# Attention queries from five products, the head sum from rounded parts, and steps of two units

## The chip, the cores and the metric

The kernel runs on one core of one Trainium2 chip. A core has five engines with a queue of instructions each, which they work off in order: TensorE (PE, matrix products), VectorE (DVE), ScalarE (ACT), GpSimd (POOL) and SyncE (SP, which here only issues DMAs). They wait for each other through semaphores. The measure is the device time of one execution in microseconds (us); lower is better.

## The reference, cut to what matters

Four layers follow each other: a state space layer (Mamba), a sparse feed forward layer, a latent attention layer, and a clustered dense layer. The change touches the attention layer. It has 4 sequences of 256 tokens, 32 heads, query latents of 192 and key/value latents of 64 numbers per token:

```
q_c = hidden_size @ Wq_c.T + bq_c
q = (q_c @ Wq_up.T + bq_up).reshape(b, s, NH, Q_HEAD).transpose(0, 2, 1, 3)
kv = hidden_size @ Wkv_c.T + bkv_c
kv_nope, kv_rope = (kv[..., :KV_LORA], kv[..., KV_LORA:])
kvu = (kv_nope @ Wkv_up.T + bkv_up).reshape(b, s, NH, QK_NOPE + V_HEAD).transpose(0, 2, 1, 3)
k_nope, v = (kvu[..., :QK_NOPE], kvu[..., QK_NOPE:])
```

Scores are softmaxed over the keys, the heads' outputs are summed over the heads, and Wo projects the sum.

## The kernel before, in words

Activations lie with features on partitions and the 1024 tokens along the free axis, in halves of 512 (h). Most products are split: an operand is kept as a rounded part (type fp32r, "high") and a rest ("low"), and three fast products, high with high, low with high, high with low, take the place of one plain f32 product. `split` writes such threes; its matmuls are L583, L584, L585.

The attention layer works on 16 pairs of heads (i). For a pair, `fold` (L884) multiplies the up projections of queries and keys (four products 128x64, L890), so that scores can be made against the key latents themselves; ACT copies the result into lAB (L1359), rounds it into lABh (L1362), and POOL makes lABl (L507). `query` (L894) makes, per head of the pair and half of the tokens (j = 0 to 3, four per pair, 64 in all), a 128x512 tile of queries from 192 latents and a row of ones that carries the bias: a three over 128 rows and a three over 65 rows, six products. ACT rounds it (L1367), DVE makes its low part (L1761). All but one of the queries use the PSUM bank A, so a query waits until the one before is evacuated.

A unit (w) is one head on one sequence; a pair has 8 units (v = w modulo 8), so there are 128 units. A unit runs through: `scores` on PE (six products of 256 columns, L919, L920, L921), maximum and its negative on DVE (L1765, L1766), exponentials on ACT (L1374, two, each with a read of its sum), normalising on DVE (L1770, L1771), `turn_p` on PE (four transposes, L932), a copy on ACT (L1383), and, once for two units, `values` on PE (L948) with its copy on ACT (L1390). `sum_up` (L952) adds a pair's values over heads, two plain f32 products of 512 columns per pair (L955).

The order is written by hand: one loop over w on each engine. PE does in step w: scores(w), turn_p(w-2), in even steps values(w//2-2) with, where due, a fold (v = 2) ahead of it and sum_up (v = 0 and 4) behind it, and in odd steps a query. ACT does copy(w-2), exp(w), in even steps the value copy, then a query's rounding or the fold's copies. DVE does top(w), norm(w-1), then a query's low part. Scores(w) waits until the exponentials of unit w-2 have been read from its bank. SP loads each pair's weights once the pair before the last is done with the buffer. After the last unit, `project_out` (L959, products L965) waits for `value_sum` (L1797) on DVE.

Of the kernel before, what the change touches and what calls it, by code (L numbers as in the profile page):

```python
# [37 lines left out]
QROWS = QL - P + 1  # L38
NC = 64
# [23 lines left out]
def bass_layers(nc, d, out):  # L63
    with ExitStack() as ctx:
# [30 lines left out]
        class Room:  # L95
# [88 lines left out]
        w_h = r(2, 2, HW)  # L184
        lAB = r(2, 4, P)
        assert r.at <= chosen
# [12 lines left out]
        lABh, lABl = (v.rearrange("p a (n c) -> p a n c", n=4) for v in (woh, wol))  # L199
        qh, ql = (zh, wh), (zl, wl)  # L200
# [6 lines left out]
        oT = r(2, TOK)  # L207
# [29 lines left out]
            "dt_ps dt_v dt_set dt_abs dt_e dt_u dt_ln dt_A dt_dt dt_T logs scr rows0 rows1 sq_set "  # L237
# [3 lines left out]
            "a_in qc_ps qc kvT_ps kvT qc_h qc_l w_h0 w_h1 w_v0 w_v1 lab cb_ps cb cb_h cb_l q_ps qp ql s_ps nmx p_e p_n pT_ps pT pv_ps oT wv_ps bvs wo_ps "  # L241
# [74 lines left out]
        def _(sp):  # L316
# [56 lines left out]
            def heads_load(i):  # L373
                k = i % 2
                sp.dma_start(w_h[:, k], d["w_h"][i][:, :, 0:HW]).then_inc(s[f"w_h{k}"], 16)
                sp.dma_start(lAB[:, k, 0::2, KVL:], d["w_h"][i][:, :, HW:]).then_inc(s[f"w_h{k}"], 16)
                sp.dma_start(lAB[0:QROWS, k, 1::2, KVL:], d["w_hB"][i]).then_inc(s[f"w_h{k}"], 16)

            for n in range(NF):
# [3 lines left out]
                if n == 5:  # L383
                    sp.wait_ge(s["lab"], 1)
                    for dst, name in ((w_qc, "w_qc"), (w_kvc, "w_kvc"), (bq, "bq"), (bkv, "bkv"), (bv, "bv"), (bo, "bo"), (w_oT, "w_oT")):
                        sp.dma_start(dst, d[name]).then_inc(s["a_in"], 16)
                if n in (6, 7):
                    heads_load(n - 6)

            sp.wait_ge(s["x2"], 2)  # L390
            for i in range(NPAIR + 1):
                k = i % 2
                if 2 <= i < NPAIR:
                    sp.wait_ge(s["cb_l"], i - 1)
                    heads_load(i)
                if i:
                    if i > 2:
                        sp.wait_ge(s["wv_ps"], 2 * i - 4)
# [14 lines left out]
        def _(po):  # L413
# [90 lines left out]

            for i in range(NPAIR):
# [10 lines left out]
        def _(pe):  # L516
# [353 lines left out]
            def latent_B(h, bank):  # L870
                for k in range(KD):
                    last = mm(PS[0:QL - P, bank], w_qc[:, k, P:QL], xn[:, k, half(h)], start=(k == 0), stop=(k == KD - 1))
# [5 lines left out]
            def keys_turned():  # L878
# [3 lines left out]
                last.then_inc(s["kvT_ps"], 1)  # L882

            def fold(i):  # L884
                if i:
                    pe.wait_ge(s["cb"], i)
                pe.wait_ge(s[f"w_h{i % 2}"], 48 * (i // 2) + 48)
                w = w_h[:, i % 2]
                for n in range(4):
                    last = mm(PS[:, B, SEQ + n * KVL:SEQ + (n + 1) * KVL], w[:, n // 2, col(n % 2)], w[:, n // 2, QL + 1:HW],  # L890
                              start=True, stop=True)
                last.then_inc(s["cb_ps"], 1)

# [1031 lines left out]
```

## Time and profile before

| what | us |
|---|---|
| median of 3 runs | 2158.49 (2156.98 to 2161.08) |
| the profiled execution's own time | 2162.24 |
| its span in the trace | 2160.4 |
| PE busy in the span | 2074.7 (96%) |
| from the first scores (1714.38) to the last values (2098.39) | 384.0 |
| of it one pair of heads in the middle | 22.60 |

Times in the trace are counted from the start of the span. Matmuls overlap in their recorded durations, since they are pipelined; what a matmul costs PE is the distance from its start to the start of the next one, not its duration.

### The profile page before, as it was taken

What the parts mean: (1) busy time and instruction counts of PE and PEld (TensorE: products, weight loads), DVE (VectorE), ACT (ScalarE), POOL (GpSimd) and SP (SyncE); (2) the same over time, 40 slices, a digit from 0 to 9 for tenths busy, and PEclk for the clock granted to TensorE, in tenths of its full rate; (3) what the DMA queues carried; (4) which work ended last, traced back from release to release, by engine and by line L of the source; (5) the groups of instructions that cost most, each with busy time, mean ns of one, the idle gap of its engine ahead of it and who ended that gap; (6) DMA issues with size and microseconds to landing.
All of it is one profiled execution on the core that took longest, in us unless ns stands there. A gap on an engine that the chain in (4) does not pass through costs nothing.

```text
span 2160.4 us, 33511 instructions
## 1 busy us (share of the span) xinstructions
PE 2074.7 (96%) x12936; PEld 1665.1 (77%) x12940; DVE 1582.5 (73%) x1701; ACT 1439.5 (67%) x3108; POOL 759.0 (35%) x391
## 2 busy tenths in 40 slices
PE   6899999999999999999999999986899989999998
PEld 4788888888888888888888888874677677777764
DVE  6778788778878887878887887777433357777765
ACT  4777786777777777777677677773533357777761
POOL 2244454444454345444444445433444100000001
PEclk9999999999999999999999999998999989999999
DMA  2222222221222122222222222221222010000001
GB/s 104 108 88 87 80 108 78 77 100 69 98 83 104 69 98 88 76 91 108 70 77 104 73 98 78 98 69 31 90 90 96 20 40 17 24 18 17 18 3 39
DMA packets 49341, 155.84 MB, mean 72 GB/s; under 512 B 13856, under 2 KB 20256, under 8 KB 40736
## 3 DMA queue, kind: packets, MB, share of 16 engines
q1 hardware_dynamic: 49184, 153.70, 20.5%
q8 instruction: 104, 1.70, 0.3%
q14 instruction: 53, 0.43, 0.1%
HBM read 151.06 MB, written 2.62 MB: 71 GB/s over the span
## 4 chain that ended last, share of the span: by engine, by line
PE 90%; DVE 7%; ACT 2%; issue 1%; DMA 0%; SPq 0%; DVEq 0%; ACTq 0%
PE PS L583 20%; PE PS L585 19%; PE PS L584 19%; PE PS L641 6%; PE PS L824 4%; PE PS L948 3%; PE PS L617 3%; PE PS L637 3%; PE PS L932 2%; PE PS L577 2%; PE PS L919 2%; PE PS L955 2%; PE PS L921 1%; PE PS L920 1%; DVE arena L1533 1%
## 5 line engine op out<-in xcount | busy, mean ns | idle before, releaser
L583 PE MATMUL PS<-xnh,wh 128*128 128x512 f32 x1272 | 510.3, 401 | 8.9 <-DVE xnl L1496 6.1
L585 PE MATMUL PS<-xnh,wl 128*128 128x512 f32 x1272 | 497.4, 391 | 0.0
L584 PE MATMUL PS<-xnl,wh 128*128 128x512 f32 x1272 | 496.5, 390 | 0.0
L1533 DVE SCALAR_TENSOR_TENSOR arena<-PS,arena 128x1020 f32<-128x1020 f32 (+2 forms) x240 | 305.6, 1273 | 31.2 <-ACT arena L1152 25.5
L1113 ACT ACTIVATE PS<-x,arena 128x128 f32<-128x128 f32 x1024 | 307.9, 354 | 22.6 <-DVE arena L1565 20.2
L583 PEld LDWEIGHTS PS<-xnh,wh 128*128 128x128 f32 x1272 | 239.6, 188 | 63.7 <-issue 14.7
L439 POOL TENSOR_TENSOR zl<-arena,zh 128x1024 fp32r<-128x1024 f32 x63 | 176.4, 2800 | 295.1 <-ACT zh L1135 295.1
L585 PEld LDWEIGHTS PS<-xnh,wl 128*128 128x128 f32 x1272 | 239.3, 188 | 52.1
L584 PEld LDWEIGHTS PS<-xnl,wh 128*128 128x128 f32 x1272 | 240.0, 189 | 46.1
L435 POOL TENSOR_TENSOR arena<-arena 128x1024 f32<-128x1024 f32 x63 | 152.0, 2412 | 296.7 <-ACT arena L1131 296.7
L424 POOL TENSOR_TENSOR wl<-arena,wh 128x1024 fp32r<-128x1024 f32 x72 | 174.8, 2428 | 200.3 <-ACT wh L1105 200.3
L583 PE MATMUL PS<-zh,woh 128*128 128x512 f32 x496 | 194.1, 391 | 0.0
L584 PE MATMUL PS<-zl,woh 128*128 128x512 f32 x496 | 194.1, 391 | 0.0
L585 PE MATMUL PS<-zh,wol 128*128 128x512 f32 x496 | 194.0, 391 | 0.0
L1571 DVE TENSOR_TENSOR sq<-sq,PS 128x1024 f32<-128x1024 f32 x124 | 150.7, 1220 | 43.3 <-PE PS L585 43.1
L641 PE MATMUL PS<-arena 128*64 128x128 f32 x2048 | 170.9, 277 | 4.4 <-DVE arena L1565 4.4
L1556 DVE TENSOR_TENSOR arena<-PS,arena 128x1024 f32<-128x1024 f32 x64 | 78.4, 1225 | 132.1 <-PE PS L617 132.1
L1765 DVE TENSOR_REDUCE arena<-PS 128x2 f32<-128x512 f32 x128 | 88.6, 693 | 113.4 <-PE PS L921 112.2
L1148 ACT ACTIVATE arena<-PS 128x1024 f32<-128x1024 f32 x64 | 65.7, 1027 | 148.6 <-PE PS L585 148.6
L1563 DVE TENSOR_TENSOR arena<-PS,arena 128x1024 f32<-128x1024 f32 x128 | 156.1, 1219 | 3.7 <-ACT PS L1117 1.5
L1124 ACT ACTIVATE PS<-x,arena 128x128 f32<-128x128 f32 x512 | 153.8, 357 | 2.2 <-DVE arena L1563 2.2
L641 PEld LDWEIGHTS PS<-arena 128*64 128x64 f32 x2048 | 120.6, 137 | 27.1 <-issue 27.1
(237 smaller groups left out, 4132.9 us busy)
## 6 DMA issues: line engine op xcount, KB each, us to landing
x<-decay SPq DMA_DIRECT2D x64, 1024.0 KB, 4.6
arena<-in_w_xg SPq DMA_DIRECT2D x72, 512.0 KB, 5.5
arena<-in_w_o SPq DMA_DIRECT2D x32, 512.0 KB, 3.4
arena<-in_w_f SPq DMA_DIRECT2D x28, 512.0 KB, 3.4
arena<-in_w_h SPq DMA_DIRECT2D x16, 257.0 KB
x<-in_x SPq DMA_DIRECT2D x3, 1024.0 KB, 7.4
out<-x SPq DMA_DIRECT2D x8, 256.0 KB, 2.0
x<-in_x SPq DMA_DIRECT2D x2, 512.0 KB, 4.2
```

Of the source, the lines that this page charges most:

```text
L424: nc.gpsimd.tensor_tensor(wl[:, k], w_raw, wh[:, k].bitcast(F32), ALU.subtract).then_inc(s["wlo"], 1)
L435: nc.gpsimd.tensor_tensor(sumsq, sumsq, ysq, ALU.add).then_inc(s["ssq"], 1)
L439: nc.gpsimd.tensor_tensor(zl[:, k], zt[:, k], zh[:, k].bitcast(F32), ALU.subtract).then_inc(s["zlo"], 1)
L583: mm(PS[:, bank], ah, bh, start=(n == 0), stop=False)
L584: mm(PS[:, bank], ah, bl, start=False, stop=False)
L585: last = mm(PS[:, bank], al, bh, start=False, stop=(n == len(terms) - 1))
L641: last = mm(PS[H, YB + u // 4, col(u % 4)], xdt[:, u, H], ring[:, hh, col(u)], start=(u % 2 == 0), stop=True)
L1113: last = act(PS[:, LB + u // 4, col(u % 4)], rowB[:, 2 * k + hh, col(u)], ACT.Relu, scale=-1.0, bias=aT[:, u, 2 * t + hh:2 * t + hh + 1])
L1124: last = act(PS[:, LB + b // 2, col(2 * hh + b % 2)], rowB[:, 2 * k + hh, col(2 * b + 1)], ACT.Exp, bias=fromend[:, k, b, hh:hh + 1])
L1533: ins = stt(o, pair_of(bank).rearrange("p q (b t) -> p q b t", t=SEQ)[:, :, :, :SEQ - k], w[:, 3 - k:4 - k], o, ALU.mult, ALU.add)
L1563: tt(both(ring[:, hh]), pair_of(LB), both(by[:, 0:TOK]), ALU.mult).then_inc(s["used"], 1)
L1571: tt(both(sq[:, m]), both(sq[:, m]), pair_of(bank), ALU.add).then_inc(s["oacc"], 1)
```

## The change

1. **Queries from five products.** The latents 128 to 191 are made twice, on partitions 0 to 63 and 64 to 127 (`latent_B` issues eight products, in place of four, on two column halves). In lABh the rows 64 to 127 of the second block now hold the low part of the weights (POOL writes it there), so that high with high and low with high of the second block are one product over 128 rows. The row of ones and the row of the bias go.
2. **Bias at evacuation.** `fold_bias` makes, per pair, two products of one column (64 values of bias for each head), and ACT copies them to biasT. ACT's rounding of a query is an Identity with that bias (before: a Copy), DVE's low part a SCALAR_TENSOR_TENSOR that adds the bias (before: a TENSOR_TENSOR). The memsets of lAB and of the row of ones go. The biases are loaded by four more small DMAs, and a pair's weights by five in place of three.
3. **Head sum from rounded parts.** ACT rounds w_v (`values_high`, 128x128, in the step with v = 6) and POOL makes its rest (`values_low`, 128x128); the value copy writes a rounded oTh, and DVE makes oTl (`value_low`, 128x256, for every two units). `sum_up` is three fp32r products in place of one f32 product.
4. **POOL.** Per pair it has three instructions in place of one: `values_low(i-2)`, then the low parts of the first blocks (128x256), then those of the second (64 partitions x 256). `values_low(i-2)` stands first and waits for `values_high` in the step v = 6, so the other two run there as well.
5. **Steps of two units.** PE does for even w: scores(w), scores(w+1), fold or fold_bias where due, values, sum_up where due, turn_p(w-2), turn_p(w-1), query. ACT does exp(w), waits for the values, fold or bias copies, value copy, values_high, copy(w-2), exp(w+1), copy(w-1), query. DVE keeps its order, with value_low behind the normalising in odd steps.
6. In the first layer some semaphores are merged.

```diff
             def query(i, j):
                 h, hh = divmod(j, 2)
-                pe.wait_ge(s["cb_l"], i + 1)
+                pe.wait_ge(s["cb_l"], 2 * i + 2)
...
-                split(query_bank(i, j), [(lABh[:, k, a], lABl[:, k, a], qcAh[:, half(h)], qcAl[:, half(h)]),
-                          (lABh[R, k, b], lABl[R, k, b], qcBh[R, half(h)], qcBl[R, half(h)])]).then_inc(s["q_ps"], 1)
+                mm(to, lABh[:, k, a], qcAh[:, half(h)], start=True, stop=False)
+                mm(to, lABh[:, k, a], qcAl[:, half(h)], start=False, stop=False)
+                mm(to, lABl[:, k, a], qcAh[:, half(h)], start=False, stop=False)
+                mm(to, lABh[:, k, b], qcBh[:, half(h)], start=False, stop=False)
+                mm(to, lABh[R, k, b], qcBl[R, half(h)], start=False, stop=True).then_inc(s["q_ps"], 1)
...
+            def fold_bias(i, at):
+
+                w = w_h[:, i % 2]
+                for hh in range(2):
+                    last = mm(PS[0:KVL, B, at + hh:at + hh + 1], w[:, hh, 2 * P + 1:], w[:, hh, 2 * P:2 * P + 1], start=True, stop=True)
+                last.then_inc(s["qb_ps"], 1)
...
             def sum_up(i, h):
-                pe.wait_ge(s[f"w_v{i % 2}"], 16 * (i // 2) + 16)
-                pe.wait_ge(s["oT"], NB * i + 2 * h + 2)
-                mm(PS[:, Y0 + h], w_v[:, i % 2], oT[:, i % 2, half(h)], start=(i == 0), stop=(i == NPAIR - 1))\
-                    .then_inc(s["wv_ps"], 1)
+                k = i % 2
+                pe.wait_ge(s["wvl"], i + 1)
+                pe.wait_ge(s["oT_l"], NB * i + 2 * h + 2)
+                mm(PS[:, Y0 + h], wvh[:, k], oTh[:, half(h)], start=(i == 0), stop=False)
+                mm(PS[:, Y0 + h], wvl[:, k], oTh[:, half(h)], start=False, stop=False)
+                mm(PS[:, Y0 + h], wvh[:, k], oTl[:, half(h)], start=False, stop=(i == NPAIR - 1)).then_inc(s["wv_ps"], 1)
...
             for i in range(NPAIR):
                 po.wait_ge(s["cb_h"], i + 1)
-                nc.gpsimd.tensor_tensor(lABl[:, i % 2], lAB[:, i % 2], lABh[:, i % 2].bitcast(F32), ALU.subtract)\
+                if i:
+                    po.wait_ge(s["cb_l"], 2 * i)
+                if i >= 2:
+                    values_low(i - 2)
+                k, R = i % 2, slice(QB, P)
+                nc.gpsimd.tensor_tensor(lABl[:, k, 0::2], lAB[:, k, 0::2], lABh[:, k, 0::2].bitcast(F32), ALU.subtract)\
                     .then_inc(s["cb_l"], 1)
-
+                po.wait_ge(s["cb_l"], 2 * i + 1)
+                nc.gpsimd.tensor_tensor(lABh[R, k, 1::2], lAB[R, k, 1::2], lABh[R, k, 1::2].bitcast(F32), ALU.subtract)\
+                    .then_inc(s["cb_l"], 1)
...
+            for w in range(0, NV + 6, 2):
                 i, v = divmod(w, 2 * NB)
-                if 2 <= w < NV + 2:
-                    copy(w - 2)
                 if w < NV:
                     exp(w)
...
+                if 4 <= w < NV + 4:
+                    ac.wait_ge(s["pv_ps"], w // 2 - 1)
+                if v == fold_step(i) and i + 2 < NPAIR:
+                    fold(i + 2)
+                elif v == fold_step(i) + 2 and i + 2 < NPAIR:
+                    fold_bias(i + 2, SEQ)
+                if 4 <= w < NV + 4:
+                    value(w // 2 - 2)
+                if v == 6 and i < NPAIR:
+                    values_high(i)
+                if 2 <= w < NV + 2:
+                    copy(w - 2)
+                if w < NV:
+                    exp(w + 1)
```

How PE's queue stands in the middle of the layer, in the step with a head sum (v = 0). Before: transposes (L932), values (L948), head sum (L955), scores of the next unit (L919 to L921), transposes, query (L583 and on).

```order
L932 MATMUL PS<-cst,arena 128x128 x4
L948 MATMUL PS<-arena 64x256 x4
L955 MATMUL PS<-arena 128x512
L919 MATMUL PS<-xnh,zh 128x256
L920 MATMUL PS<-xnl,zh 128x256
L921 MATMUL PS<-xnh,zl 128x256
L919 MATMUL PS<-xnh,zh 128x256
L920 MATMUL PS<-xnl,zh 128x256
L921 MATMUL PS<-xnh,zl 128x256
L932 MATMUL PS<-cst,arena 128x128 x4
L583 MATMUL PS<-xnh,woh 128x512
```

The same place after the change, from the end of the second unit's scores (L966): values (L997), head sum (L1005 to L1007), the transposes of two units (L977), query (L945 to L949).

```order
L966 MATMUL PS<-xnh,zl 128x256
L997 MATMUL PS<-arena 64x256 x4
L1005 MATMUL PS<-xnh,wol 128x512
L1006 MATMUL PS<-xnh,wol 128x512
L1007 MATMUL PS<-xnl,wol 128x512
L977 MATMUL PS<-cst,arena 128x128 x8
L945 MATMUL PS<-xnh,woh 128x512
L946 MATMUL PS<-xnl,woh 128x512
L947 MATMUL PS<-xnh,wol 128x512
L948 MATMUL PS<-xnh,woh 128x512
L949 MATMUL PS<-xnl,woh 128x512
```

The scores of both units now stand together ahead of the values, and both groups of transposes behind them.

ACT's queue in the step with a fold (v = 2), before: two exponentials (L1374), value copy (L1390), the fold's copies (L1359, L1362), transposes' copy (L1383), exponentials of the next unit.

```order
L1374 ACTIVATE arena<-PS,arena 128x256
L1390 ACTIVATE arena<-PS 128x256 [waits s_wv_ps,s_pv_ps]
L1359 ACTIVATE arena<-PS 128x4x64 [waits s_cb_ps]
L1362 ACTIVATE woh<-arena 128x512 [waits s_w_h1,s_cb]
L1383 ACTIVATE arena<-PS 128x512 [waits s_pv_ps,s_pT_ps]
L1374 ACTIVATE arena<-PS,arena 128x256 [waits s_pT_ps,s_nmx]
```

After: exponentials (L1445), the fold's copies (L1413, L1416), value copy (L1461), transposes' copy (L1454), exponentials of the second unit.

```order
L1445 ACTIVATE arena<-PS,arena 128x256
L1413 ACTIVATE arena<-PS 128x4x64 [waits s_cb_ps,s_pv_ps]
L1416 ACTIVATE woh<-arena 128x512 [waits s_w_h1,s_cb]
L1461 ACTIVATE xnh<-PS 128x256 [waits s_wv_ps,s_pv_ps]
L1454 ACTIVATE arena<-PS 128x512 [waits s_pv_ps,s_pT_ps]
L1445 ACTIVATE arena<-PS,arena 128x256 [waits s_pT_ps,s_nmx]
```

The fold's copies moved ahead of the value copy and wait for the values (pv_ps), and the second unit's exponentials stand behind all of them.

## Rows read from the trace of the kernel before

**Rows 1.** The page: the chain that ended last, shares of the span by engine.

```profile
PE 90%; DVE 7%; ACT 2%; issue 1%; DMA 0%; SPq 0%; DVEq 0%; ACTq 0%
```

**Rows 2.** Timeline of PE in one pair: start us, duration us, engine, line, operation.

```profile
1866.85 0.28 PE L919 MATMUL PS<-xnh,wh 128*128 128x256 f32 x1
...
1868.10 1.09 PE L948 MATMUL PS<-arena 128*64 128x256 f32 x8
1869.12 0.39 PE L919 MATMUL PS<-xnh,wh 128*128 128x256 f32 x1
...
1870.62 0.39 PE L584 MATMUL PS<-xnl,woh 128*128 128x512 f32 x1
1870.85 0.40 PE L585 MATMUL PS<-xnh,wol 128*128 128x512 f32 x1
...
1871.78 0.28 PE L919 MATMUL PS<-xnh,zh 128*128 128x256 f32 x1
...
1872.49 0.60 PE L932 MATMUL PS<-cst,arena 128*128 128x128 f32 x4
...
1877.55 0.28 PE L919 MATMUL PS<-xnh,zh 128*128 128x256 f32 x1
...
1878.71 1.00 PE L890 MATMUL PS<-arena 128*128 128x64 f32 x8
1879.64 1.09 PE L948 MATMUL PS<-arena 128*64 128x256 f32 x8
```

**Rows 3.** Timeline of DVE, same pair; in brackets idle time and its releaser.

```profile
1872.70 0.69 DVE L1765 TENSOR_REDUCE arena<-PS 128x2 f32<-128x512 f32 x1 [0.87 <-PE PS L921]
1873.42 0.17 DVE L1766 TENSOR_SCALAR arena<-arena 128x2 f32<-128x2 f32 x1
...
1874.31 0.68 DVE L1761 TENSOR_TENSOR zl<-PS,zh 128x512 fp32r<-128x512 f32 x1
```

**Rows 4.** Timeline of ACT, same pair.

```profile
1873.13 0.60 ACT L1383 ACTIVATE arena<-PS 128x512 f32<-128x512 f32 x1 [0.55 <-PE PS L932]
1873.63 0.47 ACT L1374 ACTIVATE arena<-PS,arena 128x256 f32<-128x256 f32 x1
...
1874.54 0.38 ACT L1390 ACTIVATE arena<-PS 128x256 f32<-128x256 f32 x1
```

**Rows 5.** Timeline of ACT in the step with a fold.

```profile
1880.78 0.39 ACT L1390 ACTIVATE arena<-PS 128x256 f32<-128x256 f32 x1 [0.35 <-PE PS L948]
1881.06 0.38 ACT L1359 ACTIVATE arena<-PS 128x256 f32<-128x256 f32 x1
1881.47 0.63 ACT L1362 ACTIVATE woh<-arena 128x512 fp32r<-128x512 f32 x1
```

**Rows 6.** Timeline of POOL, then of DVE, just behind it.

```profile
1882.18 1.29 POOL L507 TENSOR_TENSOR wol<-arena,woh 128x512 fp32r<-128x512 f32 x1 [21.31 <-ACT woh L1362]
...
1882.41 1.08 DVE L1766 TENSOR_SCALAR arena<-arena 128x2 f32<-128x2 f32 x1
```

**Rows 7.** Timeline, nearest rows for the new operations: one-column products of PE.

```profile
2139.95 1.09 PE L1056 MATMUL PS<-cst,arena 128*64 128x1 f32 x16
2140.97 2.05 PE L1028 MATMUL PS<-arena,cst 128*128 128x128 f32 x16
```

**Rows 8.** Groups by line and form: name, shapes, count, busy us, mean ns, idle before.

```profile
L435 POOL TENSOR_TENSOR arena<-arena 128x1024 f32<-128x1024 f32 x63 | 152.0, 2412 | 296.7 <-ACT arena L1131 296.7
L1803 DVE SCALAR_TENSOR_TENSOR x<-PS,arena,x 128x512 f32<-128x512 f32 x7 | 5.1, 747 | 2.2 <-PE PS L965 1.9
```

**Rows 9.** The layer's first steps: DVE's timeline, then stretches with busy us and PEclk.

```profile
1747.36 1.71 DVE L1771 TENSOR_TENSOR arena<-arena 128x512 f32<-128x512 f32 x1
...
1745.00:1750.00 5.00, 1.95 (x14) 1.65 (x13) 3.24 (x5) 2.90 (x8) 1.26 (x1) 0.87 0.00 0
1750.00:1755.00 5.00, 5.00 (x18) 4.09 (x20) 0.93 (x3) 0.72 (x2) 0.00 (x0) 0.50 0.00 0
```

**Rows 10.** Timeline of PE at the layer's end.

```profile
2098.39 1.09 PE L948 MATMUL PS<-arena 128*64 128x256 f32 x8 [0.89 <-ACT arena L1383]
```

More of the change, by code:

```diff
@@ L871, in latent_B @@
                 for k in range(KD):
-                    last = mm(PS[0:QL - P, bank], w_qc[:, k, P:QL], xn[:, k, half(h)], start=(k == 0), stop=(k == KD - 1))
+                    for n in range(2):
+                        last = mm(PS[n * QB:(n + 1) * QB, bank], w_qc[:, k, P:QL], xn[:, k, half(h)], start=(k == 0), stop=(k == KD - 1))
                 last.then_inc(s["qc_ps"], 1)
@@ L981, in _ @@
             query(0, 1)
-            for w in range(NV + 5):
+            for w in range(0, NV + 6, 2):
                 i, v = divmod(w, 2 * NB)
@@ L988, in _ @@
                     latent_A(1, Y0)
-                if w == 1:
+                if w < NV:
+                    scores(w + 1)
+                if w == 0:
                     latent_B(1, Y1)
@@ L1001, in _ @@
                     sum_up(i - 1, v // 4)
-                if w in QUERY_AT:
-                    query(*QUERY_AT[w])
+                for u in (w, w + 1):
+                    if 2 <= u < NV + 2:
+                        turn_p(u - 2)
+                for u in (w, w + 1):
+                    if u in QUERY_AT:
+                        query(*QUERY_AT[u])
             def dense(m, h):
@@ L1342, in latent_B @@
             def latent_B(h, bank):
-                R = slice(0, QROWS)
                 ac.wait_ge(s["qc_ps"], 3 * h + 2)
-                act(qcB[0:QL - P, half(h)], PS[0:QL - P, bank], ACT.Identity, bias=bq[0:QL - P, 1:2]).then_inc(s["qc"], 1)
+                act(qcB[:, half(h)], PS[:, bank], ACT.Identity, bias=bqB[:, 1:2]).then_inc(s["qc"], 1)
                 ac.wait_ge(s["qc"], 3 * h + 2)
-                ac.wait_ge(s["lab"], 2)
-                act(qcBh[R, half(h)], qcB[R, half(h)], ACT.Copy).then_inc(s["qc_h"], 1)
+                act(qcBh[:, half(h)], qcB[:, half(h)], ACT.Copy).then_inc(s["qc_h"], 1)
             def latent_kv(h, bank):
@@ L1366, in query @@
                 ac.wait_ge(s["q_ps"], 4 * i + j + 1)
-                act(qh[i % 2][:, hh, half(h)], PS[:, query_bank(i, j)], ACT.Copy).then_inc(s["qp"], 1)
+                ac.wait_ge(s["qb"], i + 1)
+                act(qh[i % 2][:, hh, half(h)], PS[:, query_bank(i, j)], ACT.Identity, bias=biasT[:, hh * NPAIR + i:hh * NPAIR + i + 1])\
+                    .then_inc(s["qp"], 1)
             def exp(w):
@@ L1387, in value @@
                 ac.wait_ge(s["pv_ps"], g + 1)
-                if i >= 2:
-                    ac.wait_ge(s["wv_ps"], 2 * i - 4 + b // 2 + 1)
-                act(oT[:, i % 2, b * SEQ:(b + 1) * SEQ], PS[:, B, 0:SEQ], ACT.Copy).then_inc(s["oT"], 1)
-            ac.wait_ge(s["a_in"], 16 * 7)
+                if i:
+                    ac.wait_ge(s["wv_ps"], 2 * i - 2 + b // 2 + 1)
+                act(oTh[:, b * SEQ:(b + 1) * SEQ], PS[:, B, 0:SEQ], ACT.Copy).then_inc(s["oT"], 1)
+            ac.wait_ge(s["a_in"], 16 * 11)
             fold(0)
@@ L1402, in _ @@
             query(0, 1)
-            for w in range(NV + 5):
+            for w in range(0, NV + 6, 2):
                 i, v = divmod(w, 2 * NB)
-                if 2 <= w < NV + 2:
-                    copy(w - 2)
                 if w < NV:
@@ L1782, in _ @@
             query(0, 1)
-            for w in range(NV + 1):
+            for w in range(NV + 5):
                 if w < NV:
                     top(w)
-                if w:
+                if 0 < w <= NV:
                     norm(w - 1)
+                if w >= 5 and w % 2:
+                    value_low((w - 5) // 2)
                 if w == 1:
```

126 lines of the change are left out of this document (87 added, 39 removed).

## The prediction

> **What bounds the kernel now.** I read three views in this order. The chain that ended last runs through PE for 90% of the span [rows 1], so the first question is always what PE does. The timeline of PE in one pair of heads [rows 2] shows how: in the middle of the attention layer each group of matmuls starts where the one before leaves off. A pair repeats after 22.60 us: POOL's one instruction per pair took 1.29 us behind 21.31 us of idle time [rows 6]. The timelines of DVE and ACT [rows 3 to 5] show both idle for part of each unit, waiting for PE. So a microsecond taken from PE's products is a microsecond gained, as long as the loop through DVE and ACT doesn't come up behind it.
>
> Distances between starts in [rows 2] give the prices on PE. Scores of one unit: 1871.78 to 1872.49, 0.71. One fp32r product of a query: 1870.62 to 1870.85, 0.23. Values: 1868.10 to 1869.12, 1.02, and about 0.1 each before and behind, 1.2. Fold: 1878.71 to 1879.64, 0.93, of which 0.1 is that entry into the values, so 0.83. Two units without extras: 1866.85 to 1871.78, 4.93. Two units with a head sum: 1871.78 to 1877.55, 5.77, so a head sum costs 0.84. A pair is then 4 x 4.93 + 2 x 0.84 + 0.83 = 22.2, and the period 22.6: about 0.3 per pair is PE waiting. That wait has a place. POOL's subtraction started at 1882.18 and lasted 1.29, and DVE's two-element L1766, 0.17 elsewhere [rows 3], took 1.08, to the same end [rows 6]; the exponentials and PE follow late.
>
> **The change part by part, for the steady part (all but the layer's first eight units).**
> - *Five products for six.* 0.23 a query. 64 queries, five of them in the first eight units, leaves 59: -13.7.
> - *Head sum.* 3 x 0.23 = 0.70 for 0.84, 32 times: -4.5.
> - *Bias products.* Two f32 products of one column per pair. The nearest row is L1056, the same 64 columns of weights and one column of data: 16 instructions from 2139.95 to 2140.97 [rows 7], 0.064 each. An f32 product counts as two instructions, as in the rows marked x8 for four products, so 4 x 0.064 = 0.26, 16 times: +4.2. The bounds are 2 and 6.
> - *Moves.* A step of two units holds the same transposes, values and scores, so nothing is added: 4.93 - 0.23 = 4.70. A pair's work on PE becomes 4 x 4.70 + 2 x 0.70 + 0.83 + 0.26 = 21.3.
> - *The wait at POOL* of step v = 2 goes with the instruction that caused it, which now runs at v = 6: 0.3 x 13: -3.9.
> - *Identity for Copy on ACT, and the STT on DVE.* The STT from PSUM took 0.75 [rows 8] against 0.68 [rows 3]: 0.07 on DVE. The Identity with a bias is bounded by 0 and 0.1 on ACT. DVE's new value_low (256 elements a partition, from PSUM) I take at 0.4, between zero and the 0.68 of 512. All this is beside PE's work while the loop below has slack. The new DMAs are small and issued a whole pair ahead.
>
> *New waits.* Time 0 is the start of scores(w). Scores of both units end at 0.7 and 1.4. DVE starts the maximum 0.92 after the scores start (1871.78 in [rows 2] to 1872.70 in [rows 3]), spends 0.72 on it, then 0.89 on the negative and the normalising of w-1 (1873.42 to 1874.31), then 0.68 on a query's low part: the maximum of w+1 starts at 3.2. The exponentials start 0.93 behind it (1872.70 to 1873.63, [rows 3, 4]), at 4.15, occupy ACT for 0.9 (1873.63 to 1874.54) and are complete at 5.2. Scores(w+3) needs them, and PE comes there at 4.70 + 0.7 = 5.4: slack 0.2 in a plain step, about 0.9 in a step with a head sum.
>  - *Step v = 2 (fold).* PE: fold to 2.27, values start at 2.37. ACT may only go on when they are read: 1.14 later (1879.64 in [rows 2] to 1880.78 in [rows 5]), at 3.5. Then 0.41 and 0.65 of fold copies (1881.06, 1881.47, [rows 5]), 0.28 of value copy, 0.50 of transposes' copy (1873.13 to 1873.63, [rows 4]): the second exponentials start at 5.35 and are complete at 6.37. PE comes to scores(w+3) at 4.70 + 0.83 + 0.71 = 6.24: it waits 0.17. 13 times: +2.2.
>  - *Step v = 6 (POOL).* Values start at 1.54; ACT's value copy ends its turn at 3.03, values_high (128 columns) about 0.25 later, and POOL starts at 3.36. No row has its three small subtractions. 1024 elements took 2.41 [rows 8], 512 took 1.29 [rows 6]: 2.2 ns for each and 0.17 fixed, hence 0.45, then 0.73, then 0.73, ending at about 3.8, 4.55 and 5.3. The bounds for one are nothing and the 1.29 of the full one. DVE's L1766 for w+1 is due at 3.95, in the second: it ends at 4.6, the exponentials are complete at 5.65, and scores(w+3), due at 5.42, wait 0.26. 14 times: +3.6. The third subtraction then meets the normalising of w and delays the next maximum by some 0.4, in front of a step with a head sum, whose slack takes it.
>
> For that last point a rule of the notes can be weighed. Besides L1766, the normalising L1771 took 1.71 in one place, 0.7 elsewhere, where it started 0.1 behind POOL's instruction [rows 9]. The Trainium skill, "SBUF — State Buffer", section "Who interferes with whom", says that VectorE's second port pair is GpSimd's own, that a tensor_scalar in its fast mode or an instruction with two SBUF inputs needs it, and that whoever comes second is blocked for the whole instruction. It speaks against three POOL instructions in a row at v = 6, and the trace agrees in both forms. Without it, one would count the third subtraction as free; the sum is the same by either, since that delay lies in slack.
>
> *The first eight units* (1714.4 to 1758.8) are full of waits, which the median pair hides: PE worked 1.95 of 5.00 us and then ran 5 us at a granted clock of 0.50, the 1.2 GHz level, [rows 9], after POOL's instruction held L1771 [rows 9]. That hold goes. But with two units a step, query (0,3) stands straight behind (0,2) and must wait until ACT and DVE have emptied bank A (0.6 + 0.7, and their queues), scores(5) wait for its low part, and (1,1) waits for (1,0) in the same way: three waits of 2 to 3 us for three before. I put this at 0, bounds -3 and +4.
>
> *The end.* value_sum stands behind value_low(63) on DVE: from the last values' start, 1.14 to ACT, 0.39 copy, 0.4 low part, 0.75 value_sum, in place of the 1.0 for which the last values [rows 10] occupy PE and after which the projection starts now: +1.8. The last pair has no queries; its steps go by the loop of DVE and ACT, which is once around for two units now: about -0.6 for each of three steps. Together 0.
>
> **Sum.** -13.7 - 4.5 + 4.2 - 3.9 + 2.2 + 3.6 + 0 + 0 = -12.1. The profiled execution took 2162.2, 3.7 above the median of the runs; I carry the difference over: 2158.5 - 12.1 = **2146.4 us**, 0.56% faster. What the measurement can tell from no change is about 0.2%, 4.3 us.
>
> **Rivals.**
> 1. *PE never waits.* The small POOL pieces miss L1766 (it is due only 0.13 behind the start of the second one) and the fold's chain is a little shorter: 5.8 more, 2140.6. For it: slack and wait are all under 0.3. Chance 0.15.
> 2. *The gain is given back.* If the second exponentials of every step come 0.45 later than I worked out (one more handover, say), the steps v = 2 and v = 6 each lose 0.45 more, 14 x 0.9 = 12, and the time is 2158. For it: the second unit's exponentials now stand behind a value copy and a copy that wait for PE. Against it: each piece comes from a row. Chance 0.13.
> 3. *Slower: POOL holds the port.* If a small subtraction costs as much as the whole one (1.29), the three hold it from 3.36 to 7.2. L1766 is then blocked to 5.9 in place of 4.6, PE waits 1.3 more, and the normalising and the next maximum come so late that the slack of the next step, 0.6, goes and about 0.5 more: 1.8 a pair x 14 = 25, less the 12 gained: 2171. It decides from about 0.8 us per small piece; below, we are in the forecast. Against it: 2.41 for 1024 and 1.29 for 512 elements, nearly proportional. Chance 0.10.
> 4. *The change doesn't do what it says*: the fifth product, which uses only 64 rows, or an fp32r sum behind f32 values costs PE a switch. In [rows 2] two f32-to-fp32r switches stand in every 4.93, and after the change the plain step has as many or fewer. A price of 0.3 for each of 64 would give 2165. Chance 0.02.
>
> **How the numbers follow.** Forecast 0.60, rivals 0.15, 0.13, 0.10, 0.02. Faster by over 0.2%: 0.60 + 0.15, plus a little of rival 2, less the forecast's own tail: 0.76. Within 0.2%: 0.12. Slower: 0.12. The forecast's own range, from the bounds of the bias products (2), of the first units (-3, +4) and of the two waits, is 2139 to 2153; the range for 8 in 10 takes in rivals 1 and 2: 2137 to 2158.
>
> **What the profile after would show.** Right: a period of 21.6 to 21.8 in place of 22.60; five starts 0.23 apart per query; POOL pieces near 0.45 and 0.73; one L1766 of about 0.8 per pair, now at v = 6; a wait of PE ahead of the second scores behind the fold. Wrong: a period above 22.2 with gaps of PE ahead of second scores in every step (rival 2), POOL pieces over 0.8 (rival 3), PE idle for more than 10 us in all in the first eight units, or a longer stretch there at the granted clock of 0.50.

## The result and the profile after

The changed kernel takes 2165.56 us in the median of 12 runs (2159.53 to 2170.22), the kernel before 2158.85 in 12 runs beside it (2156.98 to 2164.41). The ratio is 1.0023, 95% interval 1.0013 to 1.0034: slower by a quarter of a per cent, where 0.56% faster was forecast. By that ratio the change costs 5 us; the two medians stand 6.7 apart. The profiled execution took 2167.12 with a span of 2165.3, against 2162.24 and 2160.4 before: 4.9 more.

The first question is where those 4.9 lie. Three stretches of each kernel answer it: from the first scores to the scores of unit 8, from there to unit 120, and from there to the end. The columns are length, then busy us and count of PE, weight loads, DVE, ACT and POOL, then the granted clock, DMA share and GB/s. Before:

```profile
1714.40:1758.80 44.40, 38.19 (x159) 26.26 (x160) 17.38 (x37) 19.52 (x53) 1.26 (x1) 0.81 0.13 38
1758.80:2073.90 315.10, 313.20 (x2065) 244.24 (x2064) 226.44 (x505) 227.08 (x699) 16.77 (x13) 1.00 0.07 18
2073.90:2160.40 86.50, 72.61 (x467) 41.30 (x465) 50.58 (x78) 28.45 (x68) 6.03 (x4) 0.99 0.07 25
```

After:

```profile
1715.50:1758.40 42.90, 35.98 (x165) 22.95 (x165) 17.40 (x39) 19.96 (x56) 1.15 (x2) 0.88 0.16 42
1758.40:2074.30 315.90, 315.90 (x2090) 237.75 (x2089) 237.23 (x560) 233.41 (x725) 30.35 (x42) 1.00 0.09 22
2074.30:2165.30 91.00, 74.62 (x470) 43.06 (x469) 52.58 (x84) 29.20 (x70) 6.47 (x5) 0.96 0.07 24
```

The middle, where 12 us were to be gained, went from 315.1 to 315.9. PE is now busy in all of it, and was in 313.2 of it before: the waits of before are gone, but so is the saving of 64 products. The first units gained 1.5, the end lost 4.5, and the layer began 1.1 later. The last of these is scatter as far as the traces show: experiment two leaves the layers ahead as they were, and its first scores start at 1711.26, 3.1 before those of the kernel before. The pair of heads repeats after 22.63 us, by POOL's first instruction of two pairs in a row (1847.54 and 1870.17), against 22.60 [rows 6]:

```profile
1847.54 0.46 POOL L519 TENSOR_TENSOR wol<-arena,wol 128x128 fp32r<-128x128 f32 x1 [20.35 <-ACT wol L1431]
...
1870.17 0.46 POOL L519 TENSOR_TENSOR wol<-arena,wol 128x128 fp32r<-128x128 f32 x1 [20.31 <-ACT wol L1431]
1870.59 0.74 POOL L528 TENSOR_TENSOR wol<-arena,woh 128x256 fp32r<-128x256 f32 x1
1871.41 1.08 POOL L531 TENSOR_TENSOR woh<-arena,woh 64x256 fp32r<-64x256 f32 x1
```

The timeline of PE shows what became of the sixth product. Here are the five of a query and the first scores behind them; they answer to [rows 2].

```profile
1859.06 0.48 PE L945 MATMUL PS<-xnh,woh 128*128 128x512 f32 x1
1859.37 0.39 PE L946 MATMUL PS<-xnl,woh 128*128 128x512 f32 x1
1859.60 0.40 PE L947 MATMUL PS<-xnh,wol 128*128 128x512 f32 x1
1859.84 0.39 PE L948 MATMUL PS<-xnh,woh 128*128 128x512 f32 x1
1860.16 0.49 PE L949 MATMUL PS<-xnl,woh 64*128 64x512 f32 x1
1860.58 0.39 PE L964 MATMUL PS<-xnh,wh 128*128 128x256 f32 x1
1860.80 0.28 PE L965 MATMUL PS<-xnl,wh 128*128 128x256 f32 x1
```

L947 to L948 is 0.24, the distance of the 512-column products in [rows 2] (0.23). But L948 to L949 is 0.32, L949 to the scores 0.42, and the first two scores stand 0.22 apart in place of 0.12. The one product with 64 rows costs its own 0.23 and 0.38 around it. By these distances five products cost 1.55 where six cost 1.40: the 65-row products of before started at 1871.08, 1871.32 and 1871.55, ahead of scores at 1871.78, 0.23 apart like the others. The timeline of the weight loads shows where the time goes:

```profile
1859.38 0.19 PEld L947 LDWEIGHTS PS<-xnh,wol 128*128 128x128 f32 x1
1859.61 0.19 PEld L948 LDWEIGHTS PS<-xnh,woh 128*128 128x128 f32 x1
1860.16 0.18 PEld L949 LDWEIGHTS PS<-xnl,woh 64*128 64x128 f32 x1 [0.36 <-issue]
1860.58 0.19 PEld L964 LDWEIGHTS PS<-xnh,wh 128*128 128x128 f32 x1 [0.24 <-issue]
```

The weights of L947 and L948 are loaded 0.22 and 0.23 before their own product starts, beside the product ahead. Those of the 64-row product are loaded at 1860.16, when it starts itself, and so are those of the first 128-row product behind it (1860.58), both after idle time for which the profile names no other engine (`issue`). Before the change all six were loaded ahead, also the three over 65 rows:

```profile
1870.62 0.19 PEld L585 LDWEIGHTS PS<-xnh,wol 128*128 128x128 f32 x1
1870.85 0.19 PEld L583 LDWEIGHTS PS<-xnh,woh 65*128 65x128 f32 x1
```

The Trainium skill, "TensorE: Matmul & The Clock Gate", section "The mechanism", under what overlaps and what doesn't, says that a weight load overlaps a product under way only when the two use different row groups. The trace says otherwise here: loads for the same 128 rows overlap, and it is the change from 128 rows to 64, and back, that does not. The measurement decides. The same section also lets a load go ahead when it targets a background weight buffer, which the loads for the same rows fit; it doesn't say why the change of rows should end that, and no run here shows why.

### The profile page after: what moved, and what is told of

It is laid out like the page before. It is cut to its first block and busy times, and to the rows that moved or that the text cites. A ratio compares the mean times of both kernels' runs of the same rounds, so it can differ in the third digit from the quotient of the medians.

```text
span 2165.3 us, 33987 instructions
## 1 busy us (share of the span) xinstructions
PE 2080.8 (96%) x12986; PEld 1659.6 (77%) x12990; DVE 1593.9 (74%) x1763; ACT 1447.4 (67%) x3141; POOL 773.5 (36%) x423
## 5 line engine op out<-in xcount | busy, mean ns | idle before, releaser
L1167 ACT ACTIVATE PS<-x,arena 128x128 f32<-128x128 f32 x1024 | 307.9, 355 | 22.6 <-DVE arena L1646 20.2
L610 PEld LDWEIGHTS PS<-xnh,wh 128*128 128x128 f32 x1272 | 239.6, 188 | 63.2 <-issue 14.4
L1445 ACT ACTIVATE arena<-PS,arena 128x256 f32<-128x256 f32 x256 | 119.0, 473 | 58.2 <-DVE arena L1853 58.1
```

Of the source, the lines that this page charges most:

```text
L610: mm(PS[:, bank], ah, bh, start=(n == 0), stop=False)
L1167: last = act(PS[:, LB + u // 4, col(u % 4)], rowB[:, 2 * k + hh, col(u)], ACT.Relu, scale=-1.0, bias=aT[:, u, 2 * t + hh:2 * t + hh + 1])
```

## The experiments

Each ratio is to the kernel before, run beside the experiment: its median was 2158.49 beside experiments one to four, 2162.02 beside five to eight, and 2160.19 beside nine and ten. Between these three groups ratios are compared, not times. All differences are small, at most 1.1%, but every interval given lies clear of 1.

**One: the fifth product over all rows.** Theory A: the change in the number of rows costs 0.38 us a query. Theory B: the steps of two units hold the pair at 22.6 whatever PE has to do. The edit:

```diff
-                mm(to, lABh[R, k, b], qcBl[R, half(h)], start=False, stop=True).then_inc(s["q_ps"], 1)
+                mm(to, lABh[:, k, b], qcBl[:, half(h)], start=False, stop=True).then_inc(s["q_ps"], 1)
...
-                dst, src, high = ((qcAl, qcA, qcAh), (qcBl[0:QB], qcB[0:QB], qcBh[0:QB]), (kvl, kv, kvh))[n]
+                dst, src, high = ((qcAl, qcA, qcAh), (qcBl, qcB, qcBh), (kvl, kv, kvh))[n]
```

> The changed kernel, but the fifth product of a query and its low latents run over all 128 rows (the upper 64 rows add low weights times low latents, a term that both kernels leave out). Theory A, a change of the number of rows stalls TensorE: in the changed kernel's trace the four starts around the 64-row product lie 0.33, 0.42 and 0.22 apart where 0.235, 0.233 and 0.12 stand elsewhere, 0.38 per query, 24 us for 64 queries; without it 2142 to 2148, what is left above 2141 being new waits. Theory B, the steps of two units (second exponentials late) hold the pair at 22.6 us whatever a query costs: 2160 to 2166.

Measured: 2145.77, ratio to before 0.9934 (0.9918 to 0.9950). The middle took 297.3 for the same 112 units, and a pair 21.33. Stretches as above:

```profile
1711.90:1753.60 41.70, 34.57 (x166) 23.62 (x167) 17.11 (x39) 19.44 (x54) 0.93 (x2) 0.88 0.16 44
1753.60:2050.90 297.30, 297.07 (x2090) 243.04 (x2089) 237.35 (x561) 233.52 (x726) 30.95 (x42) 1.00 0.09 23
2050.90:2143.20 92.30, 75.88 (x470) 44.16 (x468) 52.91 (x85) 29.62 (x71) 6.47 (x5) 0.93 0.06 24
```

The same five products now stand 0.23 apart, up to the scores:

```profile
1855.08 0.40 PE L948 MATMUL PS<-xnh,woh 128*128 128x512 f32 x1
1855.31 0.39 PE L949 MATMUL PS<-xnl,woh 128*128 128x512 f32 x1
1855.54 0.28 PE L964 MATMUL PS<-xnh,wh 128*128 128x256 f32 x1
1855.66 0.28 PE L965 MATMUL PS<-xnl,wh 128*128 128x256 f32 x1
```

Twice the rows in one product, no instruction more or less, and the time falls by 20 us. Theory B is out. (The time is also what I had forecast for the change as it stands, but that is in part luck: in the profiled executions the middle gained 17.8 us and the end lost 5.8, where the forecast had 12.1 and nothing.)

**Two: the same price in the kernel before.** There the second three of each query was cut from 65 rows to 64, which leaves the bias out of the queries.

```diff
-                R = slice(0, QROWS)
+                R = slice(0, QL - P)
```

> The kernel before, with the second three products of each query over 64 rows in place of 65: the row of the bias is left out. Theory A: TensorE goes from 128 rows to 64 and back once for each query, as in the changed kernel, so about 0.38 us x 64 = 24 us more: 2180 to 2186. Theory B: 64 or 65 rows cost the same: 2157 to 2161. If the price hung on each 64-row product and not on the change of rows, three of them would cost more than one: 2200 and up.

Measured: 2180.71, ratio 1.0097 (1.0080 to 1.0114), 22.2 more than the kernel before. PE's timeline around the three, and the loads of three of these weights:

```profile
1861.84 0.40 PE L585 MATMUL PS<-xnh,wol 128*128 128x512 f32 x1
1862.16 0.50 PE L583 MATMUL PS<-xnh,woh 64*128 64x512 f32 x1
1862.50 0.39 PE L584 MATMUL PS<-xnl,woh 64*128 64x512 f32 x1
1862.73 0.39 PE L585 MATMUL PS<-xnh,wol 64*128 64x512 f32 x1
1863.05 0.38 PE L919 MATMUL PS<-xnh,wh 128*128 128x256 f32 x1
1863.27 0.28 PE L920 MATMUL PS<-xnl,wh 128*128 128x256 f32 x1
...
1862.16 0.18 PEld L583 LDWEIGHTS PS<-xnh,woh 64*128 64x128 f32 x1 [0.36 <-issue]
1862.27 0.19 PEld L584 LDWEIGHTS PS<-xnl,woh 64*128 64x128 f32 x1
...
1863.05 0.19 PEld L919 LDWEIGHTS PS<-xnh,wh 128*128 128x128 f32 x1 [0.36 <-issue]
```

The distances are 0.32, 0.34, 0.23, 0.32, 0.22, together 1.43, where the same stretch took 1.05 before (1870.85 to 1871.90): again 0.1 on either side of each change of rows, 0.38 in all. Inside the three the 64-row products stand 0.23 apart, and L584's load goes ahead, 0.23 before its product; only the loads at the two changes don't. Three 64-row products cost 0.38 around them, the same as one, so the price hangs on the change and not on the number of such products: 0.19 for each of two changes. The four steps of a pair, from one unit's scores to those of the second next (v = 0, 2, 4, 6), took 6.16, 6.14, 6.15 and 5.31, for 5.77, 5.77, 6.13 and 4.93 before: 0.38 more in each but v = 4, where the kernel before waits 0.36 behind POOL and this one has that wait filled. So the middle grew by 16.8 us (331.9 for 315.1) and not by 0.38 x 56 = 21; the last stretch grew by 2.1, and some 3 us of the medians' 22.2 these two traces don't place. Theory A holds, with nothing of the changed kernel's order in it. One row fewer costs 1%.

**Three: the fifth product left out.**

```diff
-                mm(to, lABh[:, k, b], qcBh[:, half(h)], start=False, stop=False)
-                mm(to, lABh[R, k, b], qcBl[R, half(h)], start=False, stop=True).then_inc(s["q_ps"], 1)
+                mm(to, lABh[:, k, b], qcBh[:, half(h)], start=False, stop=True).then_inc(s["q_ps"], 1)
```

> The changed kernel without the fifth product of the queries (high weights times low latents of the last 64 features are left out). Theory A: the product's 0.23 and the 0.38 around it go, 39 us if TensorE stays the bound; the loop from scores over maximum and exponentials back to scores then comes up (I put it at 4.5 us for two units against 4.5 of TensorE), so 2128 to 2140. Theory B: 2158 to 2166.

Measured: 2137.67, ratio 0.9898 (0.9880 to 0.9916). 27.9 less than the changed kernel, not 39. The product itself was worth 8.1 us against experiment one, where 0.23 x 64 = 14.7 go from PE. PE is no longer busy throughout: 287.17 of 290.40 us in the middle, and it waits for the exponentials (the table of waits names ACT's L1444 ahead of the scores).

```profile
1753.50:2043.90 290.40, 287.17 (x2034) 233.21 (x2034) 236.31 (x561) 232.69 (x725) 31.20 (x42) 1.00 0.10 24
```

The four steps of a pair took 5.36, 5.24, 5.83 and 4.41, for 5.39, 5.46, 5.84 and 4.64 in experiment one. So the loop through DVE and ACT, which the prediction had as the next limit, lies just below the five products in two steps of four (v = 0 and 4), and the other two gave back the whole product: 20.84 us a pair.

**Four: steps of one unit.** Experiment one with PE and ACT in the order of the kernel before.

```diff
-            for w in range(0, NV + 6, 2):
+            for w in range(NV + 5):
                 i, v = divmod(w, 2 * NB)
                 if w < NV:
                     scores(w)
...
-                for u in (w, w + 1):
-                    if 2 <= u < NV + 2:
-                        turn_p(u - 2)
+                if 2 <= w < NV + 2:
+                    turn_p(w - 2)
+                if w % 2 == 0 and 4 <= w < NV + 4:
+                    values(w // 2 - 2, i, v)
```

> As e1_fifth_128rows, but TensorE and ScalarE go by steps of one unit in the order of the kernel before (fold and bias copies ahead of the value copy, as the shared bank asks). TensorE's work is the same. If steps of two units are worth nothing by themselves: within 4 us of e1_fifth_128rows. If the single order leaves less slack for the added work on VectorE and ScalarE: 6 to 15 us above it. If the steps of two cause waits of their own: below it by 4 or more.

Measured: 2146.75, ratio 0.9940 (0.9924 to 0.9955): equal to experiment one, but by two differences that cancel. The middle is 7.8 longer (a pair 21.92 for 21.33), the first units 2.6 shorter and the end 3.3 shorter:

```profile
1712.90:1752.00 39.10, 33.18 (x165) 22.25 (x166) 16.66 (x38) 19.65 (x54) 1.06 (x2) 0.91 0.17 47
1752.00:2057.10 305.10, 298.25 (x2089) 243.42 (x2088) 249.93 (x561) 235.10 (x727) 26.18 (x42) 1.00 0.09 22
2057.10:2146.10 89.00, 73.27 (x470) 42.47 (x468) 53.20 (x85) 28.99 (x71) 6.47 (x5) 0.97 0.07 24
```

Steps of two thus pay 0.6 us a pair here, and cost where PE isn't full. Most of the 0.6 is one wait: in the middle of this run PE waits for the normalising behind POOL's instructions, 13 times, 7.0 us in all, 0.54 each. A step without extras is 0.05 shorter in steps of two (4.64 for 4.69). Where POOL's pieces stand elsewhere, the gain is smaller (experiment six). The cost in the first units is clear of scatter: they took 41.7 to 43.5 in the five-product runs with steps of two there (experiments one, five and ten), and 38.8 to 39.1 in those with steps of one (four, six, seven and eight). The end is less so: in the kernel before and in experiment two, whose code there differs only in the rows of the last query, it took 86.5 and 88.6.

**Five and six: the head sum.** Experiment one with the plain f32 head sum (no values_high, values_low, value_low), and then the same in steps of one unit, which leaves of the whole change little but the five products and the bias at evacuation. Two things move with it. Without values_low in front of them, POOL's two other pieces run at v = 2 again. And the kernel in steps of one unit still has ACT's values_high, whose result nothing reads.

```diff
-                mm(PS[:, Y0 + h], wvh[:, k], oTh[:, half(h)], start=(i == 0), stop=False)
-                mm(PS[:, Y0 + h], wvl[:, k], oTh[:, half(h)], start=False, stop=False)
-                mm(PS[:, Y0 + h], wvh[:, k], oTl[:, half(h)], start=False, stop=(i == NPAIR - 1)).then_inc(s["wv_ps"], 1)
+                mm(PS[:, Y0 + h], w_v[:, k], oT[:, half(h)], start=(i == 0), stop=(i == NPAIR - 1)).then_inc(s["wv_ps"], 1)
```

> As e1_fifth_128rows, but the head sum is again one plain f32 product; values_high, values_low and value_low go. In the changed kernel's trace the three fp32r products cost 0.82 us of TensorE where the f32 product cost 0.84, so the middle stays at 21.3 us a pair; the end gets shorter by 1 to 2 us, as nothing stands ahead of value_sum on VectorE. So 0 to 3 us below e1_fifth_128rows. My prediction's price (0.14 for each of 32 sums) would make it 3 to 5 us slower.

Measured: 2146.17, ratio 0.9931 (0.9914 to 0.9947), the same as experiment one. My expectation was wrong in its reason: the pair went from 21.33 to 21.65, by steps of 5.54, 5.46, 6.00 and 4.64 for 5.39, 5.46, 5.84 and 4.64. Only the two steps with a head sum differ, so POOL's pieces cost PE nothing in their other place, and the three fp32r products do save 0.16 each time, close to the 0.14 of the prediction. The expectation had compared numbers that aren't counted alike: 0.82 is the three products from start to start, 0.84 the difference between a step with a sum and one without. From start to start the f32 sum takes 0.97 here (1790.34 to 1791.31):

```profile
1790.34 1.13 PE L1000 MATMUL PS<-arena 128*128 128x512 f32 x2
1791.31 1.04 PE L973 MATMUL PS<-cst,arena 128*128 128x128 f32 x8
```

The end took 90.0 for 92.3, in the direction expected.

> Queries from five products (all over 128 rows) and bias at evacuation alone, on the order of the kernel before: steps of one unit, plain head sum. TensorE's work is 22.3 - 4 x 0.23 + 0.26 = 21.6 us a pair, with a wait behind GpSimd's fold instructions of up to 0.6: 21.6 to 22.2 a pair, 6 to 13 us below the kernel before. If the added work elsewhere costs nothing in the single order it lies within 2 us of e5_single_steps (0.994 of before).

Measured: 2145.75, ratio 0.9928 (0.9911 to 0.9944), a pair 21.81. That is about 16 us below the kernel before, more than the 6 to 13 I expected. Five products and the bias, with all rows used, carry as much as the whole change with all rows used (0.9934). Against experiment five, the same work in steps of two, the pair is only 0.16 longer, not 0.59: what steps of two pay depends on where POOL's pieces stand.

**Seven and eight: adding up what paid.** Steps of one unit for units 0 to 7 and from 120 on, of two between, and value_sum(0) ahead of the last value_low; then the same with the plain head sum.

```diff
-            for w in range(0, NV + 6, 2):
+            w = 0
+            while w < NV + 6:
                 i, v = divmod(w, 2 * NB)
+                both_ = 8 <= w < 120
...
+                w += 2 if both_ else 1
...
+                if w == NV + 3:
+                    value_sum(0)
                 if w >= 5 and w % 2:
                     value_low((w - 5) // 2)
```

> As e1_fifth_128rows, with steps of one unit for the first eight units and the last pair (steps of two between), and value_sum(0) ahead of the last value_low on VectorE. From scores 0 to scores 8 e5 took 39.1 us where e1 took 41.7; from scores 120 to the last matmul e1 took 85.7, e5 82.5, the kernel before 80.0. If these add up: 4 to 8 us below e1_fifth_128rows, 0.990 to 0.992 of before. If the waits there are only shifted: within 2 us of e1.

Measured: 2137.83, ratio 0.9890 (0.9875 to 0.9906): faster than both kernels, 1.1% below the kernel before, and a little more than I expected (0.990 to 0.992). The three stretches are those of the runs they were taken from: 39.1 of experiment four, 297.4 of experiment one, and 88.5.

```profile
1712.90:1752.00 39.10, 33.18 (x166) 22.22 (x167) 16.70 (x38) 19.67 (x55) 1.08 (x2) 0.91 0.17 47
1752.00:2049.40 297.40, 297.18 (x2090) 243.15 (x2089) 237.97 (x561) 233.41 (x727) 30.69 (x42) 1.00 0.09 23
2049.40:2137.90 88.50, 74.44 (x470) 42.95 (x468) 52.87 (x85) 29.26 (x70) 6.47 (x5) 0.96 0.07 25
```

> As e7_hybrid, but with the plain head sum of e4_plain_sum. By the 0.82 against 0.84 us of a head sum it is equal to e7_hybrid within 2 us; by my prediction's price it is 4 us slower.

Measured: 2143.44, ratio 0.9919 (0.9904 to 0.9934), 5.6 above experiment seven, 4.5 of it in the middle (301.9 for 297.4). The prediction's price of the head sum (4.5) is nearer than the "equal" I expected here.

**Nine: the 64-row product first.**

```diff
-                mm(to, lABh[:, k, a], qcAh[:, half(h)], start=True, stop=False)
+                mm(to, lABh[R, k, b], qcBl[R, half(h)], start=True, stop=False)
+                mm(to, lABh[:, k, a], qcAh[:, half(h)], start=False, stop=False)
```

> The changed kernel with the 64-row product of each query issued first of the five in place of last. Theory A: the price is that of going to 64 rows and back, wherever it is done, so within 6 us of the changed kernel: 2159 to 2171. If it came from the place (the scores behind it), the time falls towards e1_fifth_128rows: 2146 to 2152.

Measured: 2165.49, ratio 1.0027 (1.0017 to 1.0036), the time of the changed kernel. The price moved with the product:

```profile
1857.27 0.49 PE L945 MATMUL PS<-xnl,woh 64*128 64x512 f32 x1
1857.69 0.50 PE L946 MATMUL PS<-xnh,woh 128*128 128x512 f32 x1
1858.03 0.40 PE L947 MATMUL PS<-xnl,woh 128*128 128x512 f32 x1
1858.27 0.39 PE L948 MATMUL PS<-xnh,wol 128*128 128x512 f32 x1
```

0.42, 0.34, then 0.24, where the first products of experiment one stand 0.31, 0.22 and 0.24 apart. From the transposes to the scores it took 2.48 (1856.25 to 1858.73), in experiment one 2.10 (1858.08 to 1860.18): 0.38 again. At neither end of the query are the 64 rows free; the places between were not tried.

**Ten: value_sum ahead of the last value_low**, on experiment one and nothing else (the last four lines of the diff of experiment seven).

> As e1_fifth_128rows, with value_sum(0) ahead of the last value_low on VectorE, steps of two units throughout. By the changed kernel's trace the projection then starts 1.7 us earlier behind the last values (1.0 for 2.7). What is beyond 1.7 us would be the granted clock: e1's end had three stretches at 0.50, which a shorter wait may spare. So 1 to 4 us below e1_fifth_128rows (0.9934 of before): 0.9916 to 0.993; if the end's loss against the kernel before (5.7 us in e1) lay all in that wait, 0.991.

Measured: 2143.27, ratio 0.9920 (0.9903 to 0.9936), 0.0014 or 3 us below experiment one, inside the range expected; the intervals overlap. The projection starts 1.91 behind the last values' start where in experiment one it took 2.73 (2076.38 to 2079.11) at the full clock. In this run that stretch ran at a granted clock of 0.50, the 1.2 GHz level, and the values took 1.97 in place of 1.09:

```profile
2077.85 1.97 PE L997 MATMUL PS<-arena 128*64 128x256 f32 x8 [0.89 <-ACT arena L1454]
2079.76 2.70 PE L1016 MATMUL PS<-arena 128*128 128x512 f32 x4
```

In experiment seven the same distance is 1.02. The wait is gone; how much of the 3 us was it and how much the clock, these runs don't separate.

## Why the prediction was wrong, point by point

- **The bound.** Right. PE is busy in 315.90 of 315.90 us of the middle, and everything that shortened PE's products there shortened the middle, until experiment three met the loop.
- **Five products for six: the step that failed.** I priced the fifth product like the other four, 0.23, and wrote -13.7. It costs 0.23 + 0.38. Five such products are 0.15 longer than six, so the term should have been about +9 for 59 queries, 22 us off. The price came from two 128-row products [rows 2]. The trace of before also has 65-row products 0.23 apart, but 65 rows and 64 are not the same thing (experiment two). Rival 4 named this very price ("uses only 64 rows ... costs PE a switch", 0.3 for each of 64, 2165) and got a chance of 0.02. It had the mechanism, a switch that the 64 rows cost PE. That it also hit the time is in part luck: the true 0.38 is more than its 0.3, and waits that it kept did not come. The trace of before held no row of a 64-row fp32r product among 128-row ones, so the price had to be bounded from both sides, and the upper bound would have turned the sign; I let the forecast rest on the lower. The profile after shows the same: the period is 22.63 with no idle time of PE, so PE's own work had grown, which none of rivals 1 to 3 has.
- **Head sum.** -4.5 was right against an f32 sum in the order of two units (0.16 a sum: 21.65 for 21.33 a pair in experiment five against one; 4.5 us in the middle of eight against seven). Against the kernel before it is worth less. Counted alike, as a step with a sum less one without, the sum took 0.84 before (5.77 - 4.93) and takes 0.75 with three products (5.39 - 4.64, experiment one): 0.09 in place of 0.14.
- **Bias products, moves, work on PE.** Near. In experiment one the bias products lengthen the values' place by 0.22 (predicted 0.26). The moves, which I put at nothing, save 0.06 a step: 4.64 where I had worked out 4.70. A pair took 21.33, of which 0.25 is a wait; I had worked out 21.3 of work, and it is 21.1.
- **Identity and STT.** Right: ACT's rounding with the bias took 0.70 for 0.60, DVE's low part 0.74 for 0.68, value_low 0.42 (taken at 0.4), all beside PE's work.
- **The new waits.** The one behind the fold was predicted at 0.17; the prediction's own times (6.37 and 6.24) give 0.13, and those for the other (5.65 and 5.42) 0.23, not 0.26, 0.9 us less in all. In the changed kernel neither is there: the middle has no idle PE. In experiment one the second scores behind the fold start 0.30 after the product ahead in place of 0.12, and the next product 0.07 late as well: 0.25. The one at POOL in step v = 6 didn't come there either. POOL's pieces took 0.46, 0.74 and 1.08 (predicted 0.45, 0.73, 0.73), but DVE's L1853 started 0.02 ahead of the second piece, not 0.13 behind it: that much of rival 1 came true. These rows are of experiment one:

```profile
1859.44 0.17 DVE L1853 TENSOR_SCALAR arena<-arena 128x2 f32<-128x2 f32 x1
...
1859.71 1.05 DVE L1858 TENSOR_TENSOR arena<-arena 128x512 f32<-128x512 f32 x1
...
1859.46 0.75 POOL L528 TENSOR_TENSOR wol<-arena,woh 128x256 fp32r<-128x256 f32 x1
1860.29 1.08 POOL L531 TENSOR_TENSOR woh<-arena,woh 64x256 fp32r<-64x256 f32 x1
```

  What was held up instead is the normalising (1.05 for 0.70), by the second piece, and then POOL's third piece by the normalising (1.08 for 0.73); both lie in slack, since PE shows no wait there. The port rule of the Trainium skill that the prediction cites ("SBUF — State Buffer", section "Who interferes with whom"), in the form for two SBUF inputs, is seen here in both directions. Rival 3 is out, though its sign, a piece over 0.8, was there: alone the pieces cost 0.46, 0.74 and 0.73 (experiment four), and PE did not wait for them in steps of two.
- **The first units.** Predicted 0 with bounds -3 and +4; measured -1.5, within them. Experiment four shows that steps of two cost 2.6 there. As forecast, the hold of the normalising went (no normalising took over 1.0 us there), and the granted clock was 0.88 over the stretch for 0.81; that these two hid the cost is likely and was not tested apart.
- **The end.** Predicted 0, measured +4.5 in the profiled runs. The +1.8 for value_sum is right: the projection starts 2.73 behind the last values (2099.01 to 2101.74), where it started 1.02 behind them before (2098.39, [rows 10], and 2099.41).

```profile
2099.01 1.09 PE L997 MATMUL PS<-arena 128*64 128x256 f32 x8 [0.94 <-ACT arena L1454]
2101.74 3.70 PE L1016 MATMUL PS<-arena 128*128 128x512 f32 x8 [1.64 <-DVE arena L1886]
```

  The gain of 0.6 a step in the last pair isn't there: from the scores of unit 120 to those of 126 it took 14.6 us for 14.4, and to the last values 24.75 for 24.45. From the start of the projection to the end of the span it took 2.6 longer. There the granted clock was lower, 0.96 over the last stretch against 0.99, which the prediction had not in its sum: it stood at 0.50 from 2116.8 to 2123.4, and PE worked 5.2 us of that, by estimate 2.6 us lost. Why it falls there in one execution and not in another I can't say from these runs; the changed kernel's runs also spread more (10.7 us between the extremes, against 7.4).

Put together, for one pair in the middle, by its four steps (from one unit's scores to those of the second next), in us:

| step | before | after | experiment one |
|---|---|---|---|
| v = 0, head sum | 5.77 | 5.76 | 5.39 |
| v = 2, fold | 5.77 | 5.85 | 5.46 |
| v = 4, head sum, bias products | 6.13 | 5.99 | 5.84 |
| v = 6, nothing extra | 4.93 | 5.03 | 4.64 |
| pair | 22.60 | 22.63 | 21.33 |

The last step shows the change at its barest: a product gone (-0.23), the price of the rows (+0.38), the moves (-0.06), together about 0.1 more, four times a pair. Against these 0.4 stand the wait of before at v = 4 (0.36, predicted 0.3) and 0.09 for each head sum, and 0.22 for the bias products goes on top: 0.08 by this count, 0.04 measured. Over the middle that is the 0.8 of the three stretches; the rest of the 4.9 is the end's 4.5 and the late start's 1.1, less 1.5 in the first units. The forecast's steady part was -12.1 and the rows alone are +22.4 (0.38 x 59); what brings the middle back to +0.8 is that the predicted waits were not there (5.8) and the moves (0.06 in 56 steps, 3.4).

## What to carry to other kernels

Removing a product only pays if the ones that stay keep the shape of their neighbours: on a full TensorE, an fp32r product of 64 rows and 512 columns among products of 128 rows cost 0.6 us, not 0.23, so fill its other rows (as here, with a term that is harmless; zeros were not tried) rather than leave them out. When a new form of an instruction has no row in the trace, give its price both ends and see whether the far end changes the sign; if it does, it belongs in the forecast's chance and not in a rival of 2%. Interleaving units more coarsely paid where the bound engine was full (0.16 to 0.59 a pair, by where POOL's pieces stood) and cost where the pipeline filled, so the order can be switched between the two, as experiment seven does.

## What the runs showed of the hardware that I had not expected

- A weight load for 128 rows overlapped the product under way that used 128 rows (0.22 to 0.23 ahead), one for 65 rows did too, and so did one for 64 rows behind another of 64. A load that changed from 128 rows to 64 or back did not: 0.38 us for one 64-row product in between (0.09 ahead, 0.19 and 0.10 behind), 0.38 for three in a row, 0.38 when it came first of its query. Whether 96 or 32 rows behave like 65 or like 64 was not tried.
- A plain f32 product of 512 columns took 0.97 us from start to start between f32 values and f32 transposes, three fp32r products in its place 0.82. As what they add to a step: 0.84 for the f32 product ahead of fp32r scores (before), 0.9 ahead of the transposes (experiment five, 5.54 - 4.64), 0.75 for the three.
- GpSimd's subtraction over 64 partitions x 256 took the time of 128 x 256: 0.73 where nothing held it (experiment four), 1.08 behind VectorE's normalising.
